# Attention scores over 32-row strips, two head groups in one burst, on one Trainium2 core

## The reference: what is computed

```
wq = (LN(x) @ wq_w.T + wq_b).reshape(b, t, 16, 8)      # 16 heads of 8 features
wk = (ctx @ wk_w.T + wk_b).reshape(b, t, 16, 8)
wv = (ctx @ wv_w.T + wv_b).reshape(b, t, 16, 8)
probs = softmax(einsum('bthd,bshd->bhts', wq, wk) / sqrt(8), axis=-1)
attn = einsum('bhts,bshd->bthd', probs, wv)            # then @ wo_w.T + wo_b
x = x + tanh(g_xattn[0]) * attn
x = x + tanh(g_ffn[0]) * moe(LN(x))                    # 8 experts, the top 2 of them
...                                                    # a second attention, a second expert layer
```

## Time and profile before

| | |
|---|---|
| median of three executions | 509.1 us (509.08 to 509.9) |
| profiled execution | 511.61 us, of which the span of the trace is 509.7 |
| PE busy | 465.3 us, 91% |
| DVE busy | 398.9 us, 78% |
| ACT busy | 307.2 us, 60% |
| POOL busy | 221.7 us, 43% |

### The profile page before, as it was taken

One profiled execution on the slowest core, in us unless ns is written; L12 is line 12 of the kernel. 1 busy time (PEld: TensorE's weight loads), 2 busy tenths in 40 slices (PEclk: granted clock), 3 DMA queues, 4 the chain that ended last, 5 costly groups with the idle time before them and its releaser, 6 DMA issues.

```text
span 509.7 us, 13965 instructions
## 1 busy us (share of the span) xinstructions
PE 465.3 (91%) x4366; PEld 375.7 (74%) x4366; DVE 398.9 (78%) x1582; ACT 307.2 (60%) x750; POOL 221.7 (43%) x299
## 2 busy tenths in 40 slices
PE   2678999999999999999799999989998889889997
PEld 1356777777777677787578887768887877778996
DVE  5778899999989889687485667767799886777973
ACT  1566888877777777455356665565635447453553
POOL 4322145555554434467000177742777861214420
PEclk9999999999999999899999999998999999998999
DMA  8701011111111110134455664320100121000011
GB/s 242 306 12 53 14 32 33 42 36 37 36 36 33 33 55 22 38 105 115 115 170 167 172 177 121 104 64 18 27 21 22 53 62 43 12 0 2 1 43 41
DMA packets 45023, 34.60 MB, mean 68 GB/s; under 512 B 5922, under 2 KB 41122, under 8 KB 44708
## 3 DMA queue, kind: packets, MB, share of 16 engines
q1 hardware_dynamic: 30036, 20.55, 13.4%
q0 software_dynamic: 4128, 8.40, 6.0%
q10 hardware_dynamic: 10800, 4.92, 3.4%
HBM read 21.85 MB, written 11.99 MB: 66 GB/s over the span
## 4 chain that ended last, share of the span: by engine, by line
PE 57%; DVE 20%; issue 12%; POOL 3%; ACT 3%; SPq 2%; DMA 1%; DVEq 0%; POOLq 0%
PE bank L1717 13%; PE bank L1751 9%; PE bank L1924 5%; PE bank L2093 4%; PE bank L1906 4%; PE bank L1908 3%; PE bank L1907 3%; PE bank L2010 2%; DVE Pr L933 2%; DVE xs L1329 2%; DVE stat L839 2%; PE bank L1741 1%; DVE xn L857 1%; PE bank L1964 1%; PE bank L1785 1%
## 5 line engine op out<-in xcount | busy, mean ns | idle before, releaser
L1751 PE MATMUL bank<-QK 128*64 128x256 f32 x512 | 70.8, 399 | 9.4 <-ACT QK L626 5.8
L493 POOL DMA_INDIRECT sent<-xr,rowu x60 | 59.6, 993 | 45.2 <-DVE rowu L1052 28.4
L509 POOL DMA_INDIRECT yg<-done,gidx x64 | 64.0, 1000 | 32.1 <-issue 17.0
L468 POOL TENSOR_TENSOR ve<-mv,half 128x4 f32<-128x4 f32 (+1 forms) x40 | 8.9, 224 | 116.0 <-DVE mv L846 115.7
L638 ACT ACTIVATE PT<-bank 128x512 f32<-128x512 f32 x64 | 36.4, 602 | 33.7 <-PE bank L1717 33.0
L1751 PEld LDWEIGHTS bank<-QK 128*64 128x64 f32 x512 | 32.0, 140 | 27.8 <-ACT QK L626 7.1
L1310 DVE TENSOR_TENSOR act<-sil,bank 128x256 f32<-128x256 f32 x71 | 29.8, 420 | 28.6 <-ACT sil L688 28.0
L688 ACT ACTIVATE sil<-bank 128x256 f32<-128x256 f32 x71 | 27.2, 383 | 34.8 <-PE bank L1908 34.8
L929 DVE TENSOR_REDUCE mx<-bank 128x8 f32<-128x512 f32 x64 | 43.9, 686 | 5.3 <-PE bank L1751 4.5
L1924 PE MATMUL bank<-f0w_s,aT 128*128 x284 | 44.5, 279 | 0.9 <-DVE yb L1316 0.8
L933 DVE TENSOR_TENSOR Pr<-bank,mx 128x512 f32<-128x512 f32 x64 | 43.8, 685 | 1.7
(11 more groups left out here) (263 smaller groups left out, 1246.3 us busy)
## 6 DMA issues: line engine op xcount, KB each, us to landing
xb<-sent SPq DMA_DIRECT2D x71, 64.0 KB, 2.6
done<-yb ACTq DMA_DIRECT2D x71, 64.0 KB
cT<-ctx_t_dram SPq DMA_DIRECT2D x16, 128.0 KB
f0w_s<-f_w_dram SPq DMA_DIRECT2D x1, 2048.0 KB, 11.4
Pr<-ctx_t_dram SPq DMA_DIRECT2D x8, 256.0 KB
QK<-ctx_tok_dram SPq DMA_DIRECT2D x8, 256.0 KB
out_dram<-xs SPq DMA_DIRECT2D x8, 256.0 KB, 2.3
xs<-x_dram SPq DMA_DIRECT2D x2, 512.0 KB, 6.0
```

The source lines that it names most:

```text
L493: nc.gpsimd.indirect_dma_start(sent, bass.IndirectOffsetOnAxis(ap=rowu[:, s, 2 * k + c:2 * k + c + 1], axis=0), rows[:, c, :], None).then_ ...
L509: nc.gpsimd.indirect_dma_start(yg[:, s, j, :], None, done[0:NBH * P, :] if u < UG else done, bass.IndirectOffsetOnAxis(ap=gidx[:, s, j:j + ...
L1751: last = mm(bank[g % 2][L * b:L * (b + 1), 256 * p:256 * (p + 1)], QT[:, s, g, t:t + L], Kb[:, s, :, t:t + L], start=True, stop=True)
```

## The change

1. Queries are kept once (`QT` is 128 x 256 a unit), and a group's scores are matmuls over its own 32 partitions of queries and keys. `a_s` now issues two groups, 0 and 1 or 2 and 3, in one burst of eight matmuls, and waits for both subtracts of the pair before.
2. ACT writes the queries in one instruction instead of four, and GpSimd's memset of the copies goes (the counts of `fill` fall from 10 to 9).
3. `a_vs` moves from DVE to ACT, behind `a_xts` and `a_ats`, which change places.
4. PE's turn has a new order: `a_xt` ahead of `a_at`, both transposes of groups 2 and 3 together, `a_qk` behind `a_y`.
5. DVE's turn has a new order: groups 0 and 1, then the small work, then groups 2 and 3.

```diff
-        QT = QK[:, 0:U4 // 2, :].rearrange("p u (a t) -> p (u a) t", t=2 * P).rearrange("p (s g) t -> p s g t", s=2)
+        QT = QK[:, 0, :].rearrange("p (s t) -> p s t", s=2)
...
-            nc.gpsimd.memset(QK[:, 0:U4 // 2, :], 0.0).then_inc(fill, 1)
...
 def a_qks(u, s):
-                for g in range(NG):
-                    rows_g = slice(32 * g, 32 * (g + 1))
-                    nc.scalar.activation(QT[rows_g, s, g, :], bank[4][rows_g, 0:2 * P], ACT.Identity, bias=bqs[rows_g], scale=float(DH) ** -0.5)
+                nc.scalar.activation(QT[:, s, :], bank[4][:, 0:2 * P], ACT.Identity, bias=bqs[:], scale=float(DH) ** -0.5)
...
+            def a_vs(u, s):
+                a.wait_ge(S("a_v"), u + 1)
+                for e in range(2):
+                    keys = slice(L * e, L * (e + 1))
+                    last = nc.scalar.activation(Vb[keys, s, :, :, DH * e:DH * (e + 1)],
+                                                bank[5][keys, 0:2 * P].rearrange("p (b h d) -> p b h d", b=4, d=DH), ACT.Copy)
+                last.then_inc(S("a_vs"), 1)
...
+                if has(u + 2):
+                    a_xts(u + 2)
                 if has(u - 1):
                     a_ats(u - 1)
-                if has(u + 2):
-                    a_xts(u + 2)
+                if has(u):
+                    a_vs(u, s)
...
-            def a_s(u, s, g):
-                if g == 0:
+            def a_s(u, s, first):
+                if first == 0:
                     pe.wait_ge(S("a_qks"), u + 1)
-                wait(pe, S("a_sub"), u * 4 + (g - 1))
+                wait(pe, S("a_sub"), u * 4 + first)
                 for p in range(2):
-                    for b in range(2):
-                        t = P * p + L * b
-                        last = mm(bank[g % 2][L * b:L * (b + 1), 256 * p:256 * (p + 1)], QT[:, s, g, t:t + L],
-                                  Kb[:, s, :, t:t + L], start=True, stop=True)
-                last.then_inc(S("a_s"), 1)
+                    for g in range(2):
+                        rows_g = slice(32 * (first + g), 32 * (first + g + 1))
+                        for b in range(2):
+                            t = P * p + L * b
+                            last = mm(bank[g][L * b:L * (b + 1), 256 * p:256 * (p + 1)], QT[rows_g, s, t:t + L],
+                                      Kb[rows_g, s, :, t:t + L], start=True, stop=True)
+                        if p == 1:
+                            last.then_inc(S("a_s"), 1)
```

More of the change, by code:

```diff
@@ L418, in _ @@
                 if u == 1:
-                    sp.wait_ge(fill, 10)
+                    sp.wait_ge(fill, 9)
                     for e in range(E):
@@ L459, in _ @@
             nc.gpsimd.memset(chosen[:], 0.0).then_inc(fill, 1)
-            nc.gpsimd.memset(QK[:, 0:U4 // 2, :], 0.0).then_inc(fill, 1)
             pool.dma_start(f0g_s[:], f0_wg).then_inc(ld_f0g, 16)
-            pool.wait_ge(fill, 10)
+            pool.wait_ge(fill, 9)
             def rstd(k, u, n):
@@ L644, in _ @@
             a.wait_ge(prep, 3)
-            a.wait_ge(fill, 10)
+            a.wait_ge(fill, 9)
             def r_xts(v):
@@ L889, in _ @@
             v.wait_ge(ld_attn, 64)
-            v.wait_ge(fill, 10)
+            v.wait_ge(fill, 9)
             nc.vector.tensor_copy(bvb[:], colv[:, BV:BV + 1].to_broadcast([P, P]))
@@ L913, in split_biases @@
                 last.then_inc(S("rbias"), 1)
[L916 to L922, removed]
             def scores(g):
@@ L1246, in it_a @@
                     r_ln(u - 2, s)
-                if has(u):
-                    a_vs(u, s)
                 if has(u + 1):
@@ L1264, in it_a @@
                     t_expert()
-                if has(u + 1):
-                    a_max(u + 1, 2)
                 if isinstance(u, int) and u == UT:
                     t_before()
-                if has(u + 1):
-                    a_sub(u + 1, 1 - s, 2)
+                if has(u - 1):
+                    a_x(u - 1)
+                if has(u - 1):
+                    sums(1, u - 1, 2)
+                if has(u - 2):
+                    logits(1, u - 2, 2, bank[3][:, 2 * P:2 * P + 2 * E].rearrange("p (c e) -> p c e", e=E))
                 if isinstance(u, int) and u == UT:
@@ L1273, in it_a @@
                 if has(u - 1):
[L1274 to L1278, removed]
+                    moments(1, u - 1, 2)
                 if has(u - 2):
                     largest(1, u - 2, 2)
+                    experts(1, u - 2, 2)
                 if has(u + 1):
+                    a_max(u + 1, 2)
+                    a_sub(u + 1, 1 - s, 2)
                     a_max(u + 1, 3)
[L1283 to L1287, removed]
                     a_sub(u + 1, 1 - s, 3)
@@ L1833, in it_a @@
                     r_rank(u - 3)
+                if has(u + 2):
+                    a_xt(u + 2, s)
                 if has(u - 1):
@@ L1839, in it_a @@
                     a_s(u + 1, 1 - s, 0)
[L1840 to L1843, removed]
                 if has(u - 2):
@@ L1847, in it_a @@
                     a_pt(u, s, 2)
[L1848 to L1852, removed]
                     a_pt(u, s, 3)
@@ L1855, in it_a @@
                     a_y(u - 1)
+                if has(u + 2):
+                    a_qk(u + 2, s)
                 if has(u - 2):
@@ L1858, in it_a @@
                 if has(u + 1):
-                    a_s(u + 1, 1 - s, 3)
+                    a_s(u + 1, 1 - s, 2)
                 if has(u):
```

## The result

The changed kernel took 520.64 us (median of 4 executions, 515.79 to 523.67) against 509.1: a ratio of 1.0191, 95% interval 1.0119 to 1.0263. A ratio leaves out executions more than 1.5% above the fastest of their kernel, here the one of 523.67. It is slower, by some 2%, where 494.3 and a gain were forecast. Its profiled execution took 515.79 us, span 514.0. The forecast for the profiled execution was 496.9, so 18.9 us have to be found.

What follows compares the result with a forecast made beforehand. PE and DVE alternate in a loop of 11.64 us a turn. Gains of 11.0 (turns 3 to 13), 1.75, 1.4 and 1.0 less 0.4 make 14.75: profiled 511.6 to 496.9, median 494.3, range 488 to 503.

Steps and rivals of the forecast that it cites:

- Four tiles at once: PE score bursts: two groups on four 32-row tiles stream together in 0.87 us, a burst of about 1.05.
- Strips in turn: Rival for PE's score bursts: row strips run one after the other, burst 1.9 us, turn 11.1, total 502; chance 0.12.
- passes one by one: PE score bursts: 32-row tiles do not overlap at all, burst about 3.5 us, turn 14.5, total 547; within chance 0.07.
- The cost of ACT's work: ACT per turn: one query write at 0.56 us, two Vb copies at 0.45 each, net about -0.4; ACT stays covered.
- the rival of the lost gain: Attention turns: cT or `attT` late before queries and keys, turn back at 11.64 us, total 509, no change; chance 0.05.
- The layout of the turn: Attention stage, `att` to `att`: DVE carries the loop with one 0.47 us wait on PE; turn 10.6 instead of 11.64.
- 0.1 more, so 1.8: n + 7.07.: DVE small work between the two bunches takes 1.8 us, ending 7.07 us after the start of `att` (n).
- the rival of 0.07: Slower side, chance 0.07: 32-row tiles do not overlap, 547 us, or PE's 0.7 idle drops the clock to 1.2 GHz.
- The rival on the slower side: Attention stage slower: 32-row tiles without overlap, turn 14.5 us, total 547, or a clock fall from PE idling; chance 0.07.
- Turn 14: Late attention turn without xn work: waits for scores like the others, 10.6 us instead of 10.2, a loss of 0.4.
- Turn 11: One of two attention turns with the table's steps, longer before; given the same 1.0 us gain as turns 3 to 13.

Runs made afterwards that it cites:

- f1: e1 with scores on 64-row strips from two query copies, groups 0 and 2 then 1 and 3, small matmul before each burst: 501.17 us, ratio 0.981.
- e1: The changed kernel with GpSimd's weight subtraction moved ahead of the turn's four sends: 511.05 us, ratio 1.0011 to the kernel before.
- f2: f1 with GpSimd's subtraction back in its old place behind the sends: 511.98 us, ratio 1.0045 to the kernel before.
- c1: The kernel before with only GpSimd's subtraction moved ahead of its sends: 513.9 us, ratio 1.008.
- e4: The kernel before, old orders, one group at a time, plus single query copy, 32-row strips and values on ACT: 544.94 us, no ratio given.
- c2: e4 with 64-row strips of two query copies instead of 32-row strips of one, small matmul carrying each wait: 518.84 us, ratio 1.017.
- e3: The changed kernel with GpSimd's subtraction moved ahead of the sends and three unread matmuls in PE's wait for `chosen`: 503.88 us, ratio 0.9894.
- f3: f1 plus three unread matmuls in PE's wait for `chosen`: 500.65 us, ratio 0.9793 to the kernel before.
- g1: f1 plus unread matmuls in three long PE waits (turns -1, 0 and 12): 498.98 us, ratio 0.9802 to the kernel before.

## Why the prediction was wrong, step by step

- **Four tiles at once: right.** 16 records in 1.09, steps of (1.09 - 0.43) / 3 = 0.22, against 1.05 forecast. Strips in turn (1.9) and passes one by one (3.6) are out. The Trainium skill ("TensorE: Matmul & The Clock Gate", Part 3, measured speedup) gives 3.07 times for four row tiles of 512 columns, and by an estimate from it the streaming part would have been 1.13. This row, with two row by two column tiles of 256 columns, gives some 0.88 (4 steps of 0.22); no cost of this size shows here.
- **The cost of ACT's work: right** (0.46 and 0.38 for 0.56 and 0.45). No wait for cT, `attT` or QK held up the second bunch in turns 2 to 10; the rival of the lost gain in these waits is out.
- **The layout of the turn: right in f1**, 10.72 for 10.6, once stall and clock are away.
- **The step that failed: "0.1 more, so 1.8: n + 7.07."** The small work was summed from durations that its instructions had in their old place. The sum held their own dependences and left out what GpSimd does at the new time. Measured 3.19 in the turn shown, of which 1.25 is `kept_dif` (1.41 against 0.16). Its rows hold 5.2 of the 18.9 us. Taking the stall away brought 1.8% or some 9 us in e1 against the changed kernel, and 10.9 us in turns 3 to 10 of f1's trace against f2's, since the waits of PE that the stall makes, and the falls of the clock behind them, go with it. The rule was at hand: the Trainium skill ("SBUF — State Buffer", Who interferes with whom) says that a VectorE instruction with two SBUF inputs and a GpSimd instruction that reads SBUF lock each other out for a whole instruction. This case's traces agree, with ends 0.02 us apart here and 0.06 in c1. Here the row of `kept_dif` starts 0.11 before that of the subtraction (117.51, 117.62) and yet ends behind it, so the starts in the rows don't tell which of the two waits. The prediction asked of each moved DVE instruction when its inputs are ready, and of none what GpSimd does meanwhile.
- **The second failed step: the clock, "since PE now idles 0.7 in a turn; it stood at 1.00 with PE near full".** It stood inside the rival of 0.07, with idle time as its only cause. e4 against c2 and e3 against f3 show another, the strips of 32 rows, which does it with PE busy; f2 shows that long waits do it too. In the changed kernel the first `att` and turns 12, 14 and 15, all with falls or a late first rise, lie 8.6 us over the layout together, and turn 4 another 2.3. Once the stall is gone the clock costs more: f1 is 2.0% or 10 us below e1, where the two differ in the strips, their pairing, one more query write and the two small matmuls, the last two of which only add work.
- **The rival on the slower side** gave 547 for tiles that don't overlap; that mechanism was wrong. PE's idle time, 2.13 us here against 0.7 in the forecast, is a consequence of the stall, so the first failed step fed the second.
- **Turn 14** was forecast at 10.6 and is 10.72 in f1; 12.89 here is the clock.
- **Turn 11** was given the gain of the others ("I give them the same") and has none of it at any clock: 12.06 here and 12.07 in g1, whose clock stood at 1.00 there, against 11.16. The table's small VectorE rows fell in part into the 0.8 us of waits before (0.61 and 0.19, of which turn 11 keeps nothing) and made that turn 0.5 longer; the new turn has one wait of 0.4, keeps 0.2 of it, and gets 1.35 longer. This term was 0.9 too high.

What stays open: why the profiled execution of f1 still ends at 503.15 and not at 496.9. By the times of `att`, 2.2 of it is the start (39.80 instead of 37.55), 1.1 turns 1 and 2, 0.6 turns 3 to 10, 3.1 turns 11 to 13, and 0.4 the last two, less 1.4 behind them; g1 has a part of it back, with the waits filled. Why fewer rows bring the clock down isn't shown, only that they do. How the falls of the clock are spread over executions (496.06 to 503.19 in g1) isn't known from one trace each.

## What to carry to other kernels

When instructions of VectorE are moved, lay them out against what GpSimd does at the new time: a two-number subtraction from SBUF beside GpSimd's made a turn 1.2 us longer (11.96 in f2), and moving GpSimd's instruction away gave it back (10.72 in f1); the same cure in the old order cost 0.8%. Narrow row strips save PE time but cost clock: strips of 64 rows, two side by side, kept both: with the stall away in either, ratios of 0.981 and 1.0011. When a fix uncovers the next limit (stall, then clock, then the waits of the outer turns), test the fixes alone and together, for a stall can hide what a slow clock costs.

## What was unexpected of the hardware

- TensorE's granted clock was 0.58 over 47 us in which PE was busy 47.00, with score matmuls over 32 of the 128 rows; a like program over 64 rows had 1.00. The first full-speed burst came at 22 us with 128 rows, at 50 with 64 and at 61 with 32.
- Four tiles of 32 x 64 with 256 columns each ran as fast as two of 128 x 64: 1.09 for 16 records against 1.04 to 1.08 for 8.
- A VectorE `TENSOR_TENSOR` of 128 x 2 from SBUF lasted up to 1.47 us instead of 0.16 beside a GpSimd instruction of 1.28. In the profile this looks like work and not like a wait: the row is longer, and no idle time stands ahead of it.
